# A four-part transformer kernel on one core: the order in which its query stage begins, and which engines make the last low halves of that stage

## The reference

```python
x = x + tanh(g_xattn[0]) * L0_xattn(ctx, layernorm(x), ...)   # a sparse graph attention, by top-k
x = x + tanh(g_ffn[0])   * L0_ffn(layernorm(x), ...)          # Hadamard, 8-bit tokens, ternary weights
x = x + tanh(g_xattn[1]) * L1_xattn(layernorm(x), ctx, ...)   # latent attention, 16 heads
x = x + tanh(g_ffn[1])   * L1_ffn(layernorm(x), ...)          # gated, 8-bit tokens, ternary weights
```

```python
q_hk  = (hidden_q @ Wq.T).reshape(B, S, 16, 128)          # first product
q_big = einsum("bshk,hkq->bshq", q_hk, w_kc_q)            # second product, 384 wide
q_big = q_big * cos + rotate_half(q_big) * sin            # rotation
q_r   = einsum("bshq,hqr->bhsr", q_big, W_qr)             # third product, 64 wide
attn  = softmax(q_r @ k_r^T);  ctx_c = attn @ kv_r        # attention, then two more products
```

## Time and profile before

| | us |
|---|---|
| median of three runs (1733.31 to 1733.82) | 1733.66 |
| the profiled execution, its own time | 1735.35 |
| its span in the profile | 1733.5 |
| PE busy in the span | 1664.9 (96%) |
| DVE busy | 1502.8 (87%) |
| ACT busy | 1020.3 (59%) |
| POOL busy | 812.1 (47%) |

### The profile page before, as it was taken

One profiled execution on the slowest core, in us unless ns is written; L12 is line 12 of the kernel. 1 busy time (PEld: TensorE's weight loads), 2 busy tenths in 40 slices (PEclk: granted clock), 3 DMA queues, 4 the chain that ended last, 5 costly groups with the idle time before them and its releaser, 6 DMA issues.

```text
span 1733.5 us, 28006 instructions
## 1 busy us (share of the span) xinstructions
PE 1664.9 (96%) x9726; PEld 1174.8 (68%) x9776; DVE 1502.8 (87%) x2933; ACT 1020.3 (59%) x1863; POOL 812.1 (47%) x876
## 2 busy tenths in 40 slices
PE   8798899999998999999999899999999999999999
PEld 5576766666665766676666578778778777874443
DVE  6988889999998899999999888878887878879885
ACT  7888678878996222111111766666666665646664
POOL 3100022121222778666666676666667666655110
PEclk9999999999999999999999999999999999999999
DMA  8764116456841232323333522323223223133444
GB/s 325 264 212 165 38 56 154 123 127 164 171 120 37 74 104 76 89 68 87 81 79 97 179 75 82 86 77 86 83 70 87 81 62 80 50 121 78 92 89 106
DMA packets 157915, 186.05 MB, mean 107 GB/s; under 512 B 85584, under 2 KB 112464, under 8 KB 154576
## 3 DMA queue, kind: packets, MB, share of 16 engines
q1 hardware_dynamic: 146160, 154.58, 32.4%
q10 hardware_dynamic: 11616, 29.70, 6.2%
HBM read 110.83 MB, written 37.75 MB: 86 GB/s over the span
## 4 chain that ended last, share of the span: by engine, by line
PE 69%; DVE 23%; ACT 3%; issue 3%; POOL 2%; ACTq 0%; DMA 0%; DVEq 0%; POOLq 0%
PE ps L2614 6%; PE ps L2603 5%; PE ps L2104 4%; PE ps L2683 4%; PE ps L2737 3%; PE ps L2739 3%; PE ps L2738 3%; PE ps L444 3%; PE ps L2685 3%; PE ps L2684 3%; PE ps L2059 3%; PE ps L1646 3%; PE ps L1664 3%; PE ps L1638 3%; PE ps L2061 3%
## 5 line engine op out<-in xcount | busy, mean ns | idle before, releaser
L2653 POOL TENSOR_SCALAR E<-E,ri 128x512 f32<-128x512 f32 x250 | 387.7, 1568 | 187.6 <-DVE ri L2637 177.1
L2623 ACT ACTIVATE E<-ps,nm 128x512 f32<-128x512 f32 x256 | 175.7, 692 | 85.3 <-DVE nm L2630 85.3
L2372 POOL TENSOR_TENSOR R<-R,R 128x512 f32<-128x512 f32 x128 | 163.4, 1299 | 114.5 <-DVE R L2313 114.5
L2755 ACT ACTIVATE TH<-ps 128x512 fp32r<-128x512 f32 x256 | 140.2, 602 | 123.0 <-PE ps L2614 123.0
L2824 DVE TENSOR_TENSOR TL<-ps,TH 128x512 fp32r<-128x512 f32 x256 | 165.2, 686 | 29.0 <-ACT TH L2755 28.8
L2192 ACT ACTIVATE KH<-ps 128x512 fp32r<-128x512 f32 x64 | 38.3, 598 | 255.7 <-PE ps L2084 245.5
L2630 DVE TENSOR_REDUCE nm<-ps 128x1 f32<-128x512 f32 x256 | 162.4, 679 | 0.5 <-PE ps L2603 0.4
L1575 POOL TENSOR_SCALAR sc<-sc,gs 128x1 f32<-128x1 f32 x32 | 15.0, 469 | 310.4 <-DVE sc L1447 310.4
L2614 PE MATMUL ps<-CST,E 128*128 128x128 f32 x1024 | 134.2, 273 | 3.1 <-DVE TL L2824 1.6
L2614 PEld LDWEIGHTS ps<-CST,E 128*128 128x128 f32 x1024 | 118.8, 140 | 24.9 <-issue 3.6
L1438 DVE SCALAR_TENSOR_TENSOR U<-fTH,sc,ps 128x512 f32<-128x512 f32 x128 | 95.1, 745 | 26.6 <-PE ps L1646 19.0
(11 more groups left out here) (294 smaller groups left out, 4518.5 us busy)
## 6 DMA issues: line engine op xcount, KB each, us to landing
wr<-in_wff SPq DMA_DIRECT2D x24, 1024.0 KB, 5.5
aw<-in_wff ACTq DMA_DIRECT2D x40, 512.0 KB, 4.8
scratch<-QS SPq DMA_DIRECT2D x128, 128.0 KB, 2.4
KS<-KP SPq DMA_DIRECT2D x64, 256.0 KB, 3.6
QR<-scratch SPq DMA_DIRECT2D x64, 256.0 KB, 3.2
keys<-KST SPq DMA_DIRECT2D x32, 256.0 KB, 3.4
KR<-keys SPq DMA_DIRECT2D x30, 256.0 KB, 3.8
wscr<-awb ACTq DMA_DIRECT2D x24, 256.0 KB, 3.8
```

The lines of the kernel that those rows point to most:

```text
L2372: e.tensor_tensor(Q.r1[:, z, c, :], Q.r1[:, z, c, :], ask_r2(Q, n)[:, c, :], ALU.add).then_inc(S_["radd"].sem, 1)
L2623: e.activation(A.e[:, x % EB, :], K.PS[x % 4][:], ACT.Exp, bias=A.nm[:, c], accum_out=A.sm[:, c]).then_inc(S_["exp"].sem, 1)
L2653: e.tensor_scalar(A.e[:, x % EB, :], A.e[:, x % EB, :], A.ri[:, x % 8:x % 8 + 1], None, ALU.mult).then_inc(K.S["pl"].sem, 1)
```

## The change

Two edits. At the entry, TensorE issues the second product of item 0 ahead of the first product of item 2 and the last tile's product, and the second of item 1 ahead of the first of item 3. VectorE makes the rotation of item 0 ahead of the low half of item 2, and that of item 1 ahead of the low half of item 3.

At the exit, four low halves (items 62 and 63, pairs 29 and 30) are no longer made by VectorE. ScalarE copies the bank a second time as plain fp32 into a new tile (`Q.last`, which lies over buffers of weights and keys that are no longer needed), and GpSimd subtracts the high half from that copy. Waits that stood on the low half because of the bank (semaphores `kl` and `ql`) now stand on ScalarE's copy (`raw`, 5 to 8). The low half of pair 31, still made by VectorE, waits for `ql` 31.

```diff
@@ -1844,6 +1844,7 @@
         self.qs = at(low + 32768, [128, 2, 2, S], F32R, "QS")
         self.sv = at(low + 40960, [128, 2, S], F32R, "SV")
         self.wr = at(ub + 5120, [128, 2, 3, 128], F32, "WR")
+        self.last = [at(u + 4096 * i, [128, S], F32, f"LAST{i}") for i in range(4)]
 
 
 BY_PRODUCT = 4
@@ -2091,7 +2092,7 @@
     w.wait_ge(S_["ql"], p if p < 29 else 0)
     w.wait_ge(S_["raw"], 4)
     if p == 29:
-        w.wait_ge(S_["kl"], 63)
+        w.wait_ge(S_["raw"], 5)
     elif p == 30:
         w.wait_ge(S_["rmul"], 6 * 62 + 4)
     elif p == 31:
@@ -2118,6 +2119,42 @@
             ask_second(e, w, K, Q, step - 2)
         if step % 2 == 0:
             ask_third(e, w, K, Q, (step - 6) // 2)
+
+
+LAST_KEYS, LAST_SAVED = (62, 63), (29, 30)
+
+
+def ask_copy_key(e, w, K, Q, n):
+
+    S_ = K.S
+    w.wait_ge(S_["kh"], n + 1)
+    w.wait_ge(S_["hk"], 60)
+    e.activation(Q.last[n - 62][:], key_bank(K, n)[:], ACT.Copy).then_inc(S_["raw"].sem, 1)
+
+
+def ask_copy_saved(e, w, K, Q, p):
+
+    S_ = K.S
+    w.wait_ge(S_["qh"], p + 1)
+    w.wait_ge(S_["big"], 3 * 62 + 3)
+    e.activation(Q.last[p - 27][:], third_bank(K, p)[:], ACT.Copy).then_inc(S_["raw"].sem, 1)
+
+
+def ask_low_gpsimd(e, w, K, Q, n):
+
+    S_ = K.S
+    w.wait_ge(S_["raw"], n - 57)
+    w.wait_ge(S_["kl"], n)
+    w.wait_ge(S_["big"], 3 * n - 3)
+    e.tensor_tensor(Q.kl[:, n % 2, :], Q.last[n - 62][:], Q.kh[:, n % 2, :].bitcast(F32), ALU.subtract).then_inc(S_["kl"].sem, 1)
+
+
+def ask_saved_low_gpsimd(e, w, K, Q, p):
+
+    S_ = K.S
+    w.wait_ge(S_["raw"], p - 22)
+    w.wait_ge(S_["ql"], p)
+    e.tensor_tensor(Q.qs[:, p % 2, 1, :], Q.last[p - 27][:], Q.qs[:, p % 2, 0, :].bitcast(F32), ALU.subtract).then_inc(S_["ql"].sem, 1)
 
 
 def ask_weight(h, part):
@@ -2205,6 +2242,7 @@
 
     S_ = K.S
     w.wait_ge(S_["qh"], p + 1)
+    w.wait_ge(S_["ql"], 31 if p == 31 else 0)
     e.tensor_tensor(Q.qs[:, p % 2, 1, :], third_bank(K, p)[:], Q.qs[:, p % 2, 0, :].bitcast(F32), ALU.subtract).then_inc(S_["ql"].sem, 1)
 
 
@@ -2213,6 +2251,8 @@
     for step in steps:
         if step < 65:
             ask_high(e, w, K, Q, step - 1)
+        if step - 1 in LAST_KEYS:
+            ask_copy_key(e, w, K, Q, step - 1)
         if step == 65:
             power(e, w, K, A, 0)
             power(e, w, K, A, 1)
@@ -2221,6 +2261,8 @@
         n = step - 6
         if 0 <= n < 64 and n % 2:
             ask_saved_high(e, w, K, Q, n // 2)
+            if n // 2 in LAST_SAVED:
+                ask_copy_saved(e, w, K, Q, n // 2)
         if step == 66:
             scaled_scalar(e, w, K, A, 0)
             scaled_scalar(e, w, K, A, 1)
@@ -2329,7 +2371,7 @@
 def asks_vector(e, w, dc, K, Q, A, beside, steps):
     S_, PS = K.S, K.PS
     for step in steps:
-        if step < 65:
+        if step < 65 and step - 1 not in LAST_KEYS:
             ask_low(e, w, K, Q, step - 1)
         if step == 65:
             most(e, w, K, A, 0)
@@ -2342,7 +2384,7 @@
         if step < 67:
             ask_rotate(e, w, K, Q, step - 3)
         n = step - 6
-        if 0 <= n < 64 and n % 2:
+        if 0 <= n < 64 and n % 2 and n // 2 not in LAST_SAVED:
             ask_saved_low(e, w, K, Q, n // 2)
         if ALONE < step < 64:
             next(beside, None)
@@ -2364,6 +2406,10 @@
     for step in range(70):
         if ALONE < step < 64:
             next(beside, None)
+        if step - 1 in LAST_KEYS:
+            ask_low_gpsimd(e, w, K, Q, step - 1)
+        if step == 65:
+            ask_saved_low_gpsimd(e, w, K, Q, 29)
         n = step - 3
         if 0 <= n < 64:
             z = n % 4
@@ -2372,6 +2418,8 @@
                 e.tensor_tensor(Q.r1[:, z, c, :], Q.r1[:, z, c, :], ask_r2(Q, n)[:, c, :], ALU.add).then_inc(S_["radd"].sem, 1)
             w.wait_ge(S_["rope"], n + 1)
             e.tensor_tensor(Q.r1[:, z, 2, :], Q.r1[:, z, 2, :], ask_r2(Q, n)[:, 2, :], ALU.add).then_inc(S_["radd"].sem, 1)
+        if step == 66:
+            ask_saved_low_gpsimd(e, w, K, Q, 30)
         if step in (4, 5):
             ask_split_gpsimd(e, w, K, Q, 2 * step + 4)
             ask_split_gpsimd(e, w, K, Q, 2 * step + 5)
@@ -2588,11 +2636,11 @@
     p, j = n // 2, n % 2
     k = [A.ks, A.kp] if j else [A.kp, A.ks]
     c = slice(128 * z, 128 * z + 128)
-    w.wait_ge(S_["kl"], 64)
+    w.wait_ge(S_["raw"], 6)
     if z == 0:
         w.wait_ge(S_["ql"], 29)
     else:
-        w.wait_ge(S_["ql"], 30)
+        w.wait_ge(S_["raw"], 7)
         w.wait_ge(S_["rmul"], 6 * 63 + 4)
     w.wait_ge(S_[f"d_qf{n % 3}"], 16 * (n // 3 + 1))
     w.wait_ge(S_[f"d_ks{p % 2}"], 32 * (p // 2 + 1))
@@ -2609,7 +2657,7 @@
     w.wait_ge(S_["pl"], x + 1)
     w.wait_ge(S_["te"], x - 1)
     w.wait_ge(S_["rope"], 64)
-    w.wait_ge(S_["ql"], 31 if x else 0)
+    w.wait_ge(S_["raw"], 8 if x else 0)
     for c in range(4):
         m = e.transpose(K.PS[4 + x % 2][:, 128 * c:128 * c + 128], A.e[:, x % EB, 128 * c:128 * c + 128], K.ident)
     m.then_inc(S_["tr"].sem, 1)
@@ -3014,11 +3062,11 @@
     feed0_back(e, w, K, F, 15, 0)
     turns(10, 11)
     feed0_back(e, w, K, F, 15, 1)
+    ask_second(e, w, K, Q, 0)
     ask_first(e, w, K, Q, 2)
     feed0_down(e, w, K, F, 15)
-    ask_second(e, w, K, Q, 0)
+    ask_second(e, w, K, Q, 1)
     ask_first(e, w, K, Q, 3)
-    ask_second(e, w, K, Q, 1)
     ask_second(e, w, K, Q, 2)
     turns(12)
     ask_first(e, w, K, Q, 4)
@@ -3167,13 +3215,13 @@
     residual(e, w, dc, K, F, 14)
     ask_low(e, w, K, Q, 1)
     splits(10, 11)
+    ask_rotate(e, w, K, Q, 0)
     ask_low(e, w, K, Q, 2)
     residual(e, w, dc, K, F, 15)
     K.ends["feed0"] = dc.n
     w.wait_ge(dc.sem, dc.n)
-    ask_rotate(e, w, K, Q, 0)
+    ask_rotate(e, w, K, Q, 1)
     ask_low(e, w, K, Q, 3)
-    ask_rotate(e, w, K, Q, 1)
     ask_rotate(e, w, K, Q, 2)
     ask_low(e, w, K, Q, 4)
     ask_rotate(e, w, K, Q, 3)
```

## The result

The changed kernel takes 1736.24 us (median of 12 runs, 1734.03 to 1740.35), and in the same rounds the kernel before took 1733.48 (12 runs, 1732.34 to 1735.87). The ratio is 1.0019, with a 95% interval of 1.0011 to 1.0026: 0.11% to 0.26% slower. The profiled execution took 1736.31 us (span 1734.2), against 1735.35 (1733.5).

What follows compares the result with a forecast made beforehand. TensorE was taken to bound the query stage, so only its two ends count. Entry +2.5 us (0.8 wait, 1.7 clock) and exit −1.4 gave +1.1 on the median 1733.66: 1734.8, range 1732.2 to 1737.2.

Steps and rivals of the forecast that it cites:

- rival D: At the exit, ScalarE's second copy or GpSimd's subtraction comes late, so nothing is gained: +2.5 us, 1736.2; chance 0.10.
- Entry, wait: TensorE stands from about 545.4 to 548.05 for 12 low halves; residual 1.45 us later, item 6's first product 0.8 later.
- the 0.64: GpSimd's idle time at 570.77, waiting for ScalarE in its run before item 6; expected to go, saving 0.64 us.
- The sooner rotation: VectorE's rotation of item 0 at the entry, 8 us sooner; claimed to bring little, as its additions stand behind the factors.
- Entry, clock: TensorE's clock at its lower level from 548, behind the unfilled wait: 1.7 us taken, between 0 and 2.5.
- Exit, VectorE and GpSimd: Without the moved low halves, VectorE's rotation of 63 comes 1.7 us sooner; GpSimd's last additions end at 959.0, gain 1.4.
- The 0.3 that I took off: At the exit, GpSimd's additions of 62 end at 955.1, where those of 63 could have begun at 954.8.
- Exit, TensorE: TensorE's third product of pair 31 at 959.1 instead of 960.50, gain 1.4 us, with no clock fall counted.
- Sum: Whole change: entry +2.5 us and exit −1.4 us make +1.1 us.
- Rival B: TensorE's clock stays up at the entry: +0.8 − 1.4 = −0.6 us, 1733.0; chance 0.22.
- Rival C: Clock falls again before item 6, 1.7 us more, and the first fall costs its full 2.5: +3.6, 1737.3; chance 0.14.
- Rival E: At the entry, item 0's second product does not wait for the tiles: −3.1 us, 1730.6; chance 0.04.

Runs made afterwards that it cites:

- experiment 2: Changed kernel with 18 small matmuls filling TensorE's entry wait (1737.74 us, ratio 1.0022), then with 18 more before item 6 (1736.42 us, 1.0010).
- experiment 4: VectorE's entry order of before put back, in fill_first (1731.72 us, ratio 0.9981) and in the changed kernel (1736.06 us, 1.0012).
- experiment 6: Exit's edit alone with ScalarE's copies of pair 29 ahead of its powers (1733.74 us, 0.9996); fill_pool with 12 small matmuls before `score(0, 1)` (1730.03 us, 0.9978).
- fill_pool: fill_first with GpSimd's low halves of tiles 14 and 15 ahead of the additions of item 2; 1730.21 us, ratio 0.9968 to the kernel before.
- fill_pool_warm_exit: fill_pool with 12 small matmuls of ones in TensorE's wait before `score(0, 1)`; 1730.03 us, ratio 0.9978 to the kernel before.
- entry_only: Changed kernel with the exit's edit taken out, so the entry's reordering alone; 1740.08 us, ratio 1.0036 to the kernel before.
- warm_entry: Changed kernel with 18 small matmuls of ones in TensorE's wait ahead of item 0's second product; 1737.74 us, ratio 1.0022 to the kernel before.
- fill_first: Changed kernel with TensorE issuing item 2's first product ahead of item 0's second again; 1732.87 us, ratio 0.9994 to the kernel before.
- exit_copy_first: exit_only with ScalarE's copies of pair 29 ahead of its two powers; 1733.74 us, ratio 0.9996 to the kernel before.
- exit_only: Changed kernel with the entry's edit taken out, so the exit's edit alone; 1732.63 us, ratio 0.9994 to the kernel before.
- change_old_vector: Changed kernel with VectorE's entry order of before (rotation of item 0 behind the residual); 1736.06 us, ratio 1.0012 to the kernel before.
- fill_old_vector: fill_first with VectorE's entry order of before (rotation of item 0 behind the residual); 1731.72 us, ratio 0.9981 to the kernel before.
- warm_both: warm_entry with 18 more small matmuls in the wait ahead of item 6's first product; 1736.42 us, ratio 1.0010 to the kernel before.

## Why the prediction was right, and what in it was wrong

The forecast was 1734.8 within 1732.2 to 1737.2, and no change that can be told (0.88). The time was 1736.24, and the ratio 1.0019: a slowdown of 2.8 us by the medians, clear of zero but under the 0.2% that I had taken as the least that can be told. The direction of both parts and the two waits that carried the forecast were as predicted. The forecast time was 1.4 us too small. One term was mis-sized, the clock at the entry, and the clock at the exit had no term. That the range held was in part luck: 1736.24 is the time of rival D (1736.2), whose mechanism did not occur.

- **Entry, wait: right.** TensorE waited 2.70 (2.6 to 2.65 forecast) before 547.92. Residual 1.45 later by the wait alone: 1.55 by experiment 2. GpSimd's run 20.75 without the 0.64: 581.49 − 560.85 = 20.64. Item 6 by the wait alone +0.8: 1.55 − 0.64 − 0.11 = 0.8, where 0.11 is what that run was shorter than forecast (20.75 less 20.64). The sooner rotation brings nothing in this order: experiment 4.
- **Entry, clock: the place right, the size wrong.** I took 1.7, the loss of the row of before, and gave 2.5 as the upper end. It was 2.62 (experiment 2), since the 13 matmuls from 547.92 to 553.5 were all on the path and at half the clock. This is the step that failed: I borrowed the size from a fall in another place, though I had worked out in the same paragraph what stood at half. With 2.6 the sum at item 6 is +3.4; the profile has 3.43.
- **Exit, VectorE and GpSimd: right, a little low.** Rotation of 63 1.66 sooner (1.7), the end of the additions 1.65 (1.4). In the time of the profile before, GpSimd's subtraction of pair 29 began at 953.10 − 3.02 = 950.08 (949.9 forecast), and the additions of 63 began at 954.99 (955.1). The 0.3 that I took off was not there (experiment 6).
- **Exit, TensorE: the clock had no term.** The prediction puts it at nothing there and gives no reason. In the changed kernel it fell behind the wait of 2.05, and so it did in seven of the nine other kernels that leave this wait unfilled. It costs 0.7 at the turn (fill_pool against fill_pool_warm_exit), so the exit gave 0.91 between the profiles before and after, not 1.4 (1.30 at the third product of pair 31). But that the change brought this fall isn't shown: with the old exit and its wait of 2.52 there are two profiles, before without a fall and entry_only with one. Like beside like, the exit's edit gave 1.64 at the turn without a fall and 1.59 with one, a little more than the forecast. Rival D (nothing) is ruled out.
- **Sum.** Entry +3.23 at item 20, exit −0.91 by the two profiles, or −1.6 like beside like: +2.3 or +1.6, by the medians +2.8. What makes up the rest isn't shown.
- **Rival B** (clock up) was wrong in the profile. **Rival C** (a second fall before item 6) isn't seen in the changed kernel's profile, but its mechanism is real, if not sure: the clock fell in entry_only, warm_entry and fill_first after waits of 2.77, 2.72 and 2.76, and exit_copy_first, with the old entry, after 1.91, at a cost of 1.3 to 2.5 us to item 20. Its clause on the first fall, full 2.5, was the one that came true. Some of the 12 executions, which go up to 1740.35, may have had this second fall; only one of them has a profile, so it isn't shown. **Rival E** (no wait for the tiles) was wrong: 2.70.

**Still open.** Between 1000 and 1550 us, far behind the change, the profile after gains 1.3 us on that of before; four other kernels do so too, and the rest, exit_only and entry_only among them, don't. And the kernels without a fall there take from 107.1 to 108.9 us from item 6 to item 20 (the changed kernel 108.0), for which I have no explanation; a difference under 0.9 at item 20 means little for that reason.

## What to carry to other kernels

Before an instruction is put ahead of others in an in-order queue, ask what those others were filling: here the overtaken product was TensorE's cover for a wait that the change did not shorten, and losing it cost the wait and, more, the clock behind it. Price such a clock fall by the work that runs behind it on the path (here 13 matmuls times 0.2 us, the difference of their distances at the two levels), not by a fall seen elsewhere. Give it a chance and not a yes or no, and before a fall in one profile is put down to a change, look whether an unchanged stretch has it too. A stage waits for the last of its chains: the sooner rotation gave item 6 nothing until GpSimd's order was changed, and 1.66 us after that, of which 0.8 was left at item 20.

## What the runs showed of the hardware

- The wait of 2.70 behind the transposes of 544.62 brought a fall in all three kernels that leave it unfilled (the changed kernel, entry_only, change_old_vector). Elsewhere the same wait may or may not bring one. The old exit's wait of 2.52 brought none in the kernel before and one in entry_only (0.83 from 960 to 970). The wait of 2.05 to 2.06 us before `score(0, 1)` stands in ten kernels, the changed one among them; eight profiles have a fall behind it, two (fill_old_vector, exit_copy_first) none. Before item 6, 2.71 brought none in the changed kernel and 2.77 brought one in entry_only. The pair of 1.01 and 0.96 at the old entry brought one in the kernel before and in exit_only, and none in exit_copy_first.
- At the lower level 128x512 matmuls start 0.43 us apart, at the higher 0.23 (the kernel after, at 548.48 to 548.91 and 553.54 to 553.77).
- Small 128x128 matmuls of ones kept the clock at 1.00 in all three places where they filled a wait (windows 540 to 560 of warm_entry, 570 to 590 of warm_both, 950 to 970 of fill_pool_warm_exit).
- GpSimd's subtraction of 128x512 from SBUF takes 1.28 to 1.29 us beside a VectorE that is busy for 9.7 of 10 us, no more than in the kernel before.
